# Decoder layer with product-key experts: where the one-hot tables of two chunks are made, and in which slots

## What is computed

```
q = (xn @ w_q.T).reshape(b, s, 2, NH, KD).transpose(2, 0, 1, 3, 4)
sim = jnp.einsum('pbnhd,hkpd->pbnhk', q, keys_p)
scores, idx = jax.lax.top_k(sim, K)
all_scores = (scores[0][..., :, None] + scores[1][..., None, :]).reshape(b, s, NH, K * K)
all_idx = (idx[0][..., :, None] * NK + idx[1][..., None, :]).reshape(b, s, NH, K * K)
sc, pk = jax.lax.top_k(all_scores, K)
indices = jnp.take_along_axis(all_idx, pk, axis=-1)
wd = down[indices]
hmid = jnp.einsum('bnd,bnhkd->bnhk', inputs, wd)
hmid = jax.nn.sigmoid(sc) * jax.nn.gelu(hmid, approximate=False)
wu = up[indices]
return jnp.einsum('bnhk,bnhkd->bnd', hmid, wu)
```

## Time and profile before

| | |
|---|---|
| median of 3 runs | 3216.68 us (3213.38 to 3218.46) |
| profiled execution | 3222.22 us |
| span of its trace | 3220.3 us |
| PE (matmul) busy | 2869.4 us, 89% |
| DVE busy | 2770.1 us, 86% |
| ACT busy | 737.4 us, 23% |
| POOL busy | 599.0 us, 19% |
| mean granted clock of TensorE | 0.93 of full speed |

### The profile page before, as it was taken

The page is one execution under the profiler, slowest core; times in us unless marked ns, Lnnn a source line. Parts: engine busy times, 40 slices in busy tenths (PEclk is TensorE's granted clock), DMA queues, the critical chain, the costliest instruction groups (busy, mean ns, idle before and its releaser), DMA issues. The chain is left out here.

```text
span 3220.3 us, 81228 instructions
## 1 busy us (share of the span) xinstructions
PE 2869.4 (89%) x30692; PEld 2274.4 (71%) x30692; DVE 2770.1 (86%) x8246; ACT 737.4 (23%) x1302; POOL 599.0 (19%) x604
## 2 busy tenths in 40 slices
PE   7960067699999999999999999999999999999997
PEld 5840045477777777877787778787878777777776
DVE  5667877799989899989898989898999999898965
ACT  4720044222222222222121212121222222222210
POOL 1320000122212121212121212122221222222221
PEclk9975556899999999999999999999999999999997
DMA  5550036000000000000000000000000000000000
GB/s 169 173 143 0 0 115 208 5 5 13 14 6 11 12 12 12 12 12 11 12 12 12 12 12 12 12 12 12 12 12 12 12 12 12 12 11 12 8 8 8
DMA packets 88596, 94.14 MB, mean 29 GB/s; under 512 B 6109, under 2 KB 86910, under 8 KB 88062
## 3 DMA queue, kind: packets, MB, share of 16 engines
q1 hardware_dynamic: 88206, 88.74, 9.0%
HBM read 60.94 MB, written 27.79 MB: 28 GB/s over the span
## 5 line engine op out<-in xcount | busy, mean ns | idle before, releaser
L1009 PE MATMUL bank<-x2T,dnT 128*64 128x256 f32 x8192 | 992.3, 383 | 0.4 <-ACT gelh L1111 0.4
L959 POOL TENSOR_TENSOR hot_lo<-hot_lo,valsT 128x512 f32<-128x512 f32 x512 | 535.4, 1046 | 2441.6 <-DVE hot_lo L1216 2441.6
L1214 DVE TENSOR_TENSOR hot_hi<-iota,valsT 128x1024 f32<-128x1024 f32 x512 | 855.1, 1670 | 52.7 <-issue 36.7
L1032 PE MATMUL bank<-up,gelh 128*128 128x256 f32 x4096 | 895.8, 379 | 3.7 <-DVE gelh L1227 3.7
L1032 PEld LDWEIGHTS bank<-up,gelh 128*128 128x128 f32 x4096 | 779.1, 190 | 136.0 <-issue 28.7
L1009 PEld LDWEIGHTS bank<-x2T,dnT 128*64 128x64 f32 x8192 | 618.2, 138 | 182.2 <-issue 12.5
L1022 PEld LDWEIGHTS bank<-hot_lo,hot_hi 128*64 128x64 f32 x16384 | 584.9, 141 | 170.4 <-issue 134.4
L1022 PE MATMUL bank<-hot_lo,hot_hi 128*64 128x64 f32 x16384 | 595.9, 226 | 71.1 <-issue 39.6
L1111 ACT ACTIVATE gelh<-bank 128x512 f32<-128x512 f32 x512 | 305.7, 597 | 836.8 <-PE bank L1009 836.1
L1227 DVE TENSOR_TENSOR gelh<-bank,gelh 128x512 f32<-128x512 f32 x512 | 347.9, 680 | 83.1 <-PE bank L1022 51.8
L1216 DVE TENSOR_TENSOR hot_lo<-offs,valsT 128x512 f32<-128x512 f32 x512 | 349.7, 683 | 0.0
(11 more groups left out here) (145 smaller groups left out, 1964.2 us busy)
## 6 DMA issues: line engine op xcount, KB each, us to landing
x_scratch<-x_sb SPq DMA_DIRECT2D x64, 256.0 KB, 2.2
xT_sb<-in_xT SPq DMA_DIRECT2D x32, 256.0 KB, 2.9
x_sb<-in_x SPq DMA_DIRECT2D x32, 256.0 KB, 2.9
x_again<-x_scratch SPq DMA_DIRECT2D x32, 256.0 KB, 2.7
x_tile<-x_scratch SPq DMA_DIRECT2D x32, 256.0 KB, 3.0
x_res<-x_scratch SPq DMA_DIRECT2D x32, 256.0 KB, 2.9
out_y<-yo SPq DMA_DIRECT2D x32, 256.0 KB, 2.2
gelh<-in_table SPq DMA_DIRECT2D x4, 1024.0 KB, 8.9
```

The lines of the kernel that those rows point to most:

```text
L959: pool.tensor_tensor(hot_lo[:, q % BUFS], hot_lo[:, q % BUFS], valsT[:, par, 2, TQ * q:TQ * (q + 1), None].to_broadcast([P, TQ, 2 * CL]), ...
L1009: mm = pe.matmul(ps_h[q % 2][rows, c, :], dnT[:, k, 2 * q + c, rows], x2T[:, k, :, :].rearrange("p a t -> p (a t)"), start=(k == 0), stop= ...
L1032: mm = pe.matmul(ps_out[:, a, :], gelh[:, par, c, a, :], up[:, c, :], start=(c == 0), stop=(c == CL - 1))
L1214: dve.tensor_tensor(hot_hi[:, q % BUFS], iota[:, None, 0:P].to_broadcast([P, TQ, P]), valsT[:, par, 0, some, None].to_broadcast([P, TQ, P] ...
```

## The change

Two slots are added to the ring (`SPARE` = 2, six in all). Chunks 0 and 1 of each group use the new slots 4 and 5, the others use slot q % 4 as before. `freed_by` gives the chunk whose product on PE must be done before a hot may be written, counted from the group's first (negative numbers are chunks of the group before). Hots of chunks 3 and 4 of the next group move: they were the hots made at q = 0 and q = 1 of their own group; now that of chunk 3 is made between the two routings, and that of chunk 4 behind the second. At q = 0 and q = 1 DVE makes none. Ahead of group 0 five hots are made where three were. Room for the slots comes from five tensors of the first stage, which now end before the third begins.

```
@@ allocation @@
-        iota_i = sb("iota_i", [P, T], I32)
-        causal = sb("causal", [P, NT, P])
-        wqkv = sb("wqkv", [P, CC, 2 * GAP + HS])
-        bias = sb("bias", [2 * GAP + HS, 1])
-        proj = sb("proj", [P, C])
+        iota_i = early.enter_context(nc.sbuf_tensor("iota_i", [P, T], I32))
+        causal = early.enter_context(nc.sbuf_tensor("causal", [P, NT, P], F32))
+        wqkv = early.enter_context(nc.sbuf_tensor("wqkv", [P, CC, 2 * GAP + HS], F32))
+        bias = early.enter_context(nc.sbuf_tensor("bias", [2 * GAP + HS, 1], F32))
+        proj = early.enter_context(nc.sbuf_tensor("proj", [P, C], F32))
...
-            BUFS = 4
+            RING = 4
+            SPARE = 2
...
-            hot_hi = se("hot_hi", [P, BUFS, TQ, P])
-            hot_lo = se("hot_lo", [P, BUFS, TQ, 2 * CL])
+            hot_hi = se("hot_hi", [P, RING + SPARE, TQ, P])
+            hot_lo = se("hot_lo", [P, RING + SPARE, TQ, 2 * CL])
...
+            def slot(q):
+                return RING + q if q < SPARE else q % RING
+
+            def freed_by(q):
+                if q < SPARE:
+                    return q + 1 - NQ
+                return q + 1 - RING if q >= RING + SPARE else NQ - RING + q % RING + 1 - NQ
...
-                    if later(g, 1) or q >= BUFS:
-                        dve.wait_ge(a_mm, g * NQ + (q + 1 - BUFS))
+                    if later(g, 1) or q >= RING + SPARE:
+                        dve.wait_ge(a_mm, g * NQ + freed_by(q))
...
-                for q in range(AHEAD):
+                for q in range(AHEAD + SPARE):
                     hots(0, 0, q)
                 route(1, 0)
                 route(1, 1)
...
-                        if q + AHEAD < NQ:
+                        if SPARE <= q < NQ - AHEAD:
                             hots(g, par, q + AHEAD)
-                        elif within(g, 1):
+                        elif q >= SPARE and within(g, 1):
                             hots(g + 1, 1 - par, q + AHEAD - NQ)
...
                     if within(g, 2):
                         route(g + 2, 0)
+                    if within(g, 1):
+                        hots(g + 1, 1 - par, AHEAD)
+                    if within(g, 2):
                         route(g + 2, 1)
+                    if within(g, 1):
+                        hots(g + 1, 1 - par, AHEAD + 1)
```

More of the change, by code:

```diff
@@ L958, in gated @@
                     rest(pool, pool_rests)
-                    pool.tensor_tensor(hot_lo[:, q % BUFS], hot_lo[:, q % BUFS],
+                    pool.tensor_tensor(hot_lo[:, slot(q)], hot_lo[:, slot(q)],
                                        valsT[:, par, 2, TQ * q:TQ * (q + 1), None].to_broadcast([P, TQ, 2 * CL]),
@@ L1021, in coefs @@
                             rows = slice(half * P // 2, (half + 1) * P // 2)
-                            mm = pe.matmul(ps_a[q % 2][rows, t * 2 * CL:(t + 1) * 2 * CL], hot_hi[:, q % BUFS, t, rows],
-                                           hot_lo[:, q % BUFS, t, :], start=True, stop=True)
+                            mm = pe.matmul(ps_a[q % 2][rows, t * 2 * CL:(t + 1) * 2 * CL], hot_hi[:, slot(q), t, rows],
+                                           hot_lo[:, slot(q), t, :], start=True, stop=True)
                     mm.then_inc(a_mm, 1)
@@ L1209, in hots @@
                         dve.wait_ge(valsT_ready, g + 1)
-                    if later(g, 1) or q >= BUFS:
-                        dve.wait_ge(a_mm, g * NQ + (q + 1 - BUFS))
+                    if later(g, 1) or q >= RING + SPARE:
+                        dve.wait_ge(a_mm, g * NQ + freed_by(q))
                     rest(dve, dve_rests)
                     some = slice(TQ * q, TQ * (q + 1))
-                    dve.tensor_tensor(hot_hi[:, q % BUFS], iota[:, None, 0:P].to_broadcast([P, TQ, P]),
+                    dve.tensor_tensor(hot_hi[:, slot(q)], iota[:, None, 0:P].to_broadcast([P, TQ, P]),
                                       valsT[:, par, 0, some, None].to_broadcast([P, TQ, P]), ALU.is_equal)
-                    dve.tensor_tensor(hot_lo[:, q % BUFS], offs[:, None, :].to_broadcast([P, TQ, 2 * CL]),
+                    dve.tensor_tensor(hot_lo[:, slot(q)], offs[:, None, :].to_broadcast([P, TQ, 2 * CL]),
                                       valsT[:, par, 1, some, None].to_broadcast([P, TQ, 2 * CL]), ALU.is_equal)\
```

## The result

| | before | after |
|---|---|---|
| median of 4 runs each, taken together | 3217.57 us | 3181.30 us (3176.52 to 3185.47) |
| ratio, 95% interval | | 0.9887 [0.9876, 0.9899] |
| profiled execution | 3222.22 us | 3179.85 us |
| span of its trace | 3220.3 us | 3178.1 us |
| mean granted clock | 0.93 | 0.934 |

What follows compares the result with a forecast made beforehand. PE was taken to bound the kernel, with DVE close behind. Gains of 27.5 less 2.5 at the start made 25.0 saved; the median 3216.7 less 25.0 gave 3191.7 us, with a range of 3182 to 3207.

Steps and rivals of the forecast that it cites:

- 16 plain groups: Groups 1, 2, 3 and odd ones from 5 to 29, not behind the loop's branch: 1.02 gained each, 16.3 us.
- DVE's losses in the groups behind the branch: Groups 4, 6 to 28: five fast starters gain 5.3 us, three slow ones 1.9, the other five nothing.
- S(15): Start of PE's one-hot product of chunk 15, counted from chunk 0's; forecast 40.6 in plain groups, 41.66 before.
- start of the stage: Ahead of group 0, where no routing hides the two extra hots: 2.5 us lost.
- slow restarts behind the branch: PE restarting at 1.2 GHz in the 13 branch groups: 15 us in all, kept, plus or minus 6.
- C(1): Moment DVE is free after multiplying chunk 1 into `gelh`, from the group's start: 4.70 instead of 6.03.
- C(2): Moment DVE is free after multiplying chunk 2 into `gelh`, from the group's start: 7.28 instead of 8.95.
- 0.64 to spare: DVE's gained lead of 1.66 us per group beyond the 1.02 needed for PE to wait nowhere.
- Part of the gain: Rival: one full hold at the second routing brings DVE 1.3 later; 9.5 lost, 3201 us; chance 0.10.
- no change: Rival: PE's late steps have a second cause, such as ScalarE's GELU; 3216 us; chance 0.04.
- DVE late at its own group: Rival: both Pool operations hold DVE, 2.6 late per group; slower, 3237 us; chance 0.03.
- the two branch pauses meet: Rival: at the loop's branch code loads queue, PE's pauses grow by up to 2.8 each; 3228 us; chance 0.02.

Runs made afterwards that it cites:

- second pair: The kernel before and the changed kernel, each profiled once more without further edits; one execution each, 3218.21 us and 3178.90 us.
- after_filler: Changed kernel with useless DVE work behind the hot of chunk 4 in each group that routes; 3237.28 us, ratio 1.0044 to the kernel before.
- after_shift4: Changed kernel with four useless matmuls once, in group 1 ahead of the loop, so its PE code lies further on; 3148.86 us, ratio 0.9765.
- before_late_dve: Kernel before with about 2 us of useless DVE work ahead of the loop's branch; 3223.99 us, ratio 1.0009.
- after_longpass2: Changed kernel with useless DVE work, reckoned at about 5.5 us, ahead of the last multiplication of each odd group; 3241.16 us, ratio 1.0065.
- after_longpass1h: Changed kernel with useless DVE work, reckoned at about 3.6 us, ahead of the last multiplication of each odd group; 3223.20 us, ratio 1.0003.
- before_flat: Kernel before with the loop of 14 passes written out, so that nothing branches; 3175.75 us, ratio 0.9849.
- before_beat4: Kernel before with four more useless matmuls in the output product of each odd group; 3203.08 us, ratio 0.9938.

## Why the prediction was right in kind and too small

Against the profiled executions, 3220.3 - 3178.1 = 42.2 us of span, by the steps of the prediction:

| step | forecast | first pair of traces | second pair |
|---|---|---|---|
| 16 plain groups | 16.3 | 17.8 (16 x 1.11, from 79.88 to 78.77 per group) | 17.8 |
| DVE's losses in the groups behind the branch | 7.2 (5.3 + 1.9) | 7.2 (S(15) less the slow restart: mean 41.13 to 40.58) | 5.0 |
| group 30 | 1.7 | 1.7 (76.59 to 74.85) | 0.3 |
| group 31 | 2.3 | 2.6 (77.04 to 74.48) | 2.7 |
| start of the stage | -2.5 | -2.4 | -1.9 |
| first hot of the stage earlier or later, no effect of the change | | 1.6 | -1.7 |
| slow restarts behind the branch | 0, plus or minus 6 | 9.2 (15.4 to 6.2) | 16.5 (18.1 to 1.6) |
| pauses at the branch | 0 | 3.9 (39.6 to 35.7) | 0.0 |

The first pair sums to 41.6, with 0.6 left over; the second to 38.7 of 39.3 us. Group 30 differs since its output product, behind its wait, ran partly at 1.2 GHz in three of the four traces, and not in the second of before.

**Right.** The step from DVE's order to PE's end, in nearly every number: C(1) 4.58 (4.70 forecast), C(2) 7.23 (7.28), plain groups of 40.58 (40.6), MAX8 of 2.20 beside Pool's gating. The plain groups gained 1.11 and not 1.02: the step with the transposes is 3.29 when PE does not wait, not 3.34, and the stretch behind S(15) is 0.05 shorter. DVE comes to chunk 0 at 1.40 instead of 1.71, since the routing starts 7.35 behind S(15) and the two hots cost a little less than reckoned. The three short hots (1.22) are those of chunks 3, 4 and 5. In group 0 chunk 2 starts at 626.25, or 627.8 with the 1.6 of the earlier start added, for 628.3 forecast; the slow start behind it takes 4.80 instead of 4.37, and the two errors cancel. That the start cost came out at 2.4 for 2.5 is luck: it was reckoned from the one trace in which the routing hardly waited, and over all traces it is nearer 1.3. (For the three slow groups behind the branch the working writes 1.9, while three times its own 0.55 is 1.7.) The terms that belong to the moved hots sum to 26.9 in the first pair and 23.9 in the second, for 25.0 forecast. The 0.64 to spare is borne out by `after_filler` to 0.01. The price of DVE's pause, 2.8, was too high for the new order, where the runs show 1.4 (`after_shift4`); that changed nothing, since DVE waits for chunk 0's product anyway.

**The step that failed** is the paragraph on the clock. It kept the slow restarts at 15 us in the sum, took a new draw as even-handed, "five to eight changed ones are plus or minus 6 us", and let the range go only 10 us below the forecast. They fell to 6.2 us in the first trace and 1.6 in the second. That every pass draws anew at even chances, as it had it, does not fit the counts: there were 8 and 10 of 13 in two traces of before, 4 and 1 in two of after, and 13 of 13 in two other kernels. The Trainium skill (TensorE: Matmul & The Clock Gate, What's actually happening) says that the monitor runs free of the program. The traces agree so far as the same kernel before was slow in groups 6, 8, 12, 16, 18, 22, 26 and 28 in one trace and in 4, 8, 10, 12, 16, 18, 20, 22, 24 and 28 in the other; but I took "free" for "random in every pass". In a loop of nearly equal passes the outcomes can come in runs, up to 13 alike. By which rule is not shown. The prediction's own bound of -15 for 13 fast restarts should have been the end of the range: 3191.7 - 15 is 3177. The gain is 36.3 by the medians; with 24 to 27 of it for the order, 9 to 12 remain for the clock. This remainder is a difference, not measured in the timed executions themselves. Their granted clocks, 0.932 to 0.935 after and 0.927 to 0.932 before, point the same way.

**The rivals.** Part of the gain and no change are out: no step of 2.9 remains. DVE late at its own group did not happen (4.58, not 6.0 or more), but would have cost about what was said (`after_filler`, 2.6 late, is 14.5 above the kernel before, where the rival had 20). That the two branch pauses meet is out by `before_late_dve`: they met, and PE's did not grow.

**Taken as given, and wrong to.** The prediction left PE's pauses at the branch, 39.6 us and the slow restarts behind them, as a constant. They cost more than what the change saves: without the branch the kernel before takes 47.2 us less (3222.93 to 3175.75). Four matmuls ahead of the loop, which remove PE's pauses alone, give 31.7 of it. The Trainium skill (Runtime: NRT & Kernel Launch, Instruction fetch mechanics) says that a taken branch to a page that is not loaded costs a fetch. The runs fit that: place decides for PE, each engine has its own pause, writing the loop out ends both. No row shows a page or a fetch, so this stays the likely cause and is not shown.

**What stays open:** whether a shift of DVE's code would end its pause, and why it is half as long in the new order; by which rule a restart is slow, since passes of 163.2 to 165.0 us had only fast restarts in `after_longpass2`, while passes of 163.5 to 163.9 had only slow ones in `after_longpass1h`; and why one step of every fourth group in `before_flat` is 0.3 longer. In group 3 that step is chunk 14's, 3.21 long, and DVE's `hot_hi` beside it takes 2.09 where it takes 1.78 otherwise. None of these was tried further.

## What to carry to other kernels

When two engines are nearly equal, ask at which moment of a period the follower has its lead, and move its work into the stretch where it idles: a reordering that adds no instruction took 1.1 us out of each group that DVE had paced, and the first hot moved was worth nothing, since it had been covered already. Before tuning the inside of a loop, read what its back-branch costs on each engine, with the slow clock behind it; here it cost more than the change gained, and writing the loop out took it away. A range for a loop's slow restarts has to hold both ends, all of them slow and none. And a cost that hides behind a wait is to be read from more than one trace: the start of the stage cost 2.4 by the first pair and 1.3 over all.

## What the hardware showed that was not expected

- The same loop, four matmuls further on in PE's code, has no pause of PE at its branch, where it had 13 of 2.3 to 3.6 us; DVE's, 2.8 on average in the old order, stayed.
- More work made a kernel faster: 27.9 us of matmuls more in `before_beat4`, 19.6 us less in time.
- Restarts of PE after 2.3 to 3.6 us without work run at 2.4 GHz, or partly or wholly at 1.2 GHz, the latter in 1 to 13 of 13 passes depending on the kernel, for 1.6 to 21.6 us a run.
- Pool's gating of a hot (1.04) and 16 MAX8 from PSUM (2.20) ran beside each other with no loss to either, while hots and Pool's gating stretch each other (1.22 to 1.78 for `hot_hi`, and 1.04 to 1.86 for Pool where hots go back to back at the start).
